# Windowed attention in the last two blocks: the softmax sums divided out of a tile's outputs instead of its weights

## The chip, the cores and the metric

The kernel runs on one core of one Trainium2 chip. The metric is the device time of one execution in microseconds (us); a time given for the kernel is a median over runs. The core has five engines that each work through a queue of their own strictly in program order and wait for one another on semaphores: TensorE (PE: matmuls, and transposes, which are matmuls against an identity matrix; its weight loads are shown apart as PEld), VectorE (DVE), ScalarE (ACT), GpSimd (POOL) and SyncE (SP, which only issues DMAs here). Matmuls write to PSUM, eight banks of 128 x 512 floats; DVE and ACT read it from there.

## What is computed

The reference is a decoder of six sublayers on `x` of 4 x 512 tokens and 256 channels (an RWKV-like mixer, a quantised fusion with a context, a mixture of experts, linear attention, cross-attention, and last a stack of two windowed-attention blocks), each followed by a residual sum and a layer norm. The change touches the attention in the two blocks of the last sublayer alone. There, for each block, in short:

```python
h = shift_token(x)                       # the upper half of the channels comes from the token before
q, k, v = split(h @ wqkv, 3)             # 8 heads of 64
q = l2norm(q) * qs;  k = l2norm(k) * ksc
q, k = rotary_xpos(q, k)
sim = einsum('bhwid,bhwjd->bhwij', 8.0 * bq, bk)   # windows of 128 tokens, own keys and those of the window before
sim = where((i < j) | (i > j + 128) | (j == -1), -max, sim)
out = einsum('bhwij,bhwjd->bhwid', softmax(sim), bv)
x = x + out @ wo
... # then a gated feed-forward network (the FFN), not touched
```

A softmax divides each row of exponentials by its sum. The division may be made on the weights (128 queries x 256 keys for each head) or, since the sum belongs to a query alone, on the outputs (128 queries x 64 channels for each head).

## The kernel before

`windowed` runs the two blocks (layers) one after the other; in each, `windowed_attention` comes first and `gated_ffn` after it. The 2048 tokens are 16 tiles of 128, which is also the window; a tile is named by a unit `u` (0 to 7) and `w` (0 or 1), and `n = 2u + w` counts tiles. Tiles 0, 4, 8 and 12 begin a sequence and have no window before them: they are called alone, and their scores, exponentials, flips and combines are half as long.

The order is one list, `windowed_plan`, which all engines walk, each doing its own share of every step. `mingle(main, side)` spreads the `side` steps evenly over the `main` steps, by their counts alone. For a unit the main steps are, tile by tile, `score`, the `flip` of the tile before, `softmax`, the `combine` of the tile before, and the `output` of the tile before that; the side steps are the rotations of the next unit (`rotate`, `scale`, `turn` for q and k of both tiles) and the projections of the unit after (`project` for q, k and v of both tiles, `split`, `invert`). The steps:

- `project` (L3333 on PE, six matmuls into a bank): ACT copies the bank out (L3543). For the k part (`which == 1`) ACT also squares q and k (L3549), and DVE then sums the squares (L3441, called the reduce below).
- `invert`: ACT takes the root (L3553), for which it loads a function table and then loads that of Exp again; DVE takes the reciprocal (L3445, L3447). `rotate` is DVE's L3458 and L3461 (with POOL's share L3619, L3620), `scale` is DVE's L3469, `turn` is four transposes on PE (L3342), which ACT copies out (L3563 for k, L3568 for q). `split` is a shift on DVE (L3432) and two casts on ACT.
- `score`: PE puts the mask into banks 0 to 3 (L3354) and adds q times k (L3361). There is one set of these banks: the scores of a tile wait until ACT has read those of the tile before.
- `softmax`: DVE takes the maxima (L3480, L3482), two groups of four heads one after the other; ACT takes eight exponentials and their sums (L3580); DVE then takes the reciprocals of the sums (L3488) and scales the weights (L3491), again in two groups.
- `flip`: PE transposes the weights, sixteen blocks into four banks (L3373), and ACT and DVE copy two banks each (L3516). `combine`: PE multiplies by v, 64 channels of a head against 128 queries (L3388), and ACT copies the result into `oc` (L3594). `output`: PE multiplies `oc` by wo (L3398), and DVE adds to `x_tok` (L3502).

Banks 4 to 7 go round in the order of the plan among `project`, `turn`, `flip`, `combine` and `output` (and, near the end of a layer, the first steps of the FFN): each use waits until the use four places back has been copied out. A copy that comes late on ACT or DVE therefore holds up PE at a step that has nothing else to do with it.

Of the kernel before, what the change touches and what calls it, by code (L numbers as in the profile page):

```python
# [9 lines left out]
ALU = mybir.AluOpType  # L10
# [3 lines left out]
P = 128  # L14
# [14 lines left out]
HL, NL = 8, 64  # L29
# [3129 lines left out]
WU, UNITS_W = 2, TILES // 2  # L3159
# [5 lines left out]
def windowed_plan():  # L3165
# [20 lines left out]
    for u in range(UNITS_W):  # L3186
        main = []
        for w in range(WU):
            n, before, after = WU * u + w, [], []
            if n == LAST_W - 2:  # L3190
                before, after = GATED_FIRST[0:1], GATED_FIRST[1:2]
            elif n == LAST_W:
                before = GATED_FIRST[2:3]
            main += [("score", u, w)] + tail[0:1] + before + [("softmax", u, w)] + after + tail[1:2] + last
            last, tail = tail[2:], [("flip", u, w), ("combine", u, w), ("output", u, w)]
        rotations = rotate(u + 1) if u + 1 < UNITS_W else []
        projections = project(u + 2) if u + 2 < UNITS_W else []
        plan += mingle(main, mingle(rotations, projections))
# [53 lines left out]
def windowed_attention(m, layer, f, fs, f_use, outer):  # L3252
    nc = m.nc
    with ExitStack() as ctx:
# [15 lines left out]
        for p in plan:  # L3270
            if p[0] in ("project", "turn", "combine", "output"):
                steps.append(p)
            elif p in GATED_FIRST:
                steps += ffn_uses([p])
            elif p[0] == "flip":
                steps += [p + (g,) for g in range(len(flips(*p[1:])))]
            elif p[0] == "score":
                for x in range(2):
                    use[p + (x,)] = Use(m, 2 * x)
# [34 lines left out]
def attention_pe(m, s, t, use, plan, layer, outer, fs, f):  # L3314
    pe = m.nc.tensor
    for step in plan:
# [48 lines left out]
        elif kind == "flip":  # L3365
            w, = step[2:]
            n = WU * u + w
            for g, blocks in enumerate(flips(u, w)):
                b = use[step + (g,)]
                pe.wait_ge(*s.weighed(2 * n + blocks[0][0] // 4 + 1))  # L3370
                pe.wait_ge(*b.empty)
                for i, (x, kk) in enumerate(blocks):
                    ins = pe.transpose(b.ap[:, i * P:(i + 1) * P], t["p"][n % 2][:, x, kk * P:(kk + 1) * P], m.const("ident"))  # L3373
                ins.then_inc(*b.fill)
        elif kind == "combine":
            w, = step[2:]
# [41 lines left out]
def attention_dve(m, s, t, use, plan, layer, outer, fs, f):  # L3418
# [3 lines left out]
    for step in plan:  # L3422
# [47 lines left out]
        elif kind == "softmax":  # L3470
            w, = step[2:]
            n, lo = WU * u + w, alone(u, w) * P
            peak, total, p = t["peak"][n % 2], t["total"][n % 2], t["p"][n % 2]
            scores = m.psum[:, 0:4, :].rearrange("p b (x j) -> p (b x) j", x=2)[:, :, lo:2 * P]
# [8 lines left out]
            if n >= LAST_W - 2:  # L3483
                ffn_dve(m, fs, f, use, GATED_FIRST[n - LAST_W + 2:n - LAST_W + 3], layer)
            for x in range(2):
                h = slice(4 * x, 4 * x + 4)
                v.wait_ge(*use["score", u, w, x].done)
                v.reciprocal(total[:, h], total[:, h]).then_inc(*s.v_step.up())  # L3488
                v.wait_ge(*s.v_step.now())
                for i in range(4 * x, 4 * x + 4):  # L3490
                    ins = v.tensor_scalar(p[:, i, lo:2 * P], p[:, i, lo:2 * P], total[:, i:i + 1], None, ALU.mult)  # L3491
                ins.then_inc(*s.weighed.up())
        elif kind == "flip":
# [25 lines left out]
def attention_act(m, s, t, use, plan, layer, outer, fs, f):  # L3519
    act = m.nc.scalar  # L3520
    for step in plan:
# [47 lines left out]
        elif kind == "softmax":  # L3569
# [3 lines left out]
            if n > 1:  # L3573
                before = (n - 2) // WU, (n - 2) % WU
                act.wait_ge(*s.weighed(2 * (n - 1)))
                act.wait_ge(*use[("flip",) + before + (len(flips(*before)) - 1,)].full)
# [8 lines left out]
        elif kind == "flip":  # L3585
            w, = step[2:]
            flip_out(m, t, use, u, w, 0)
        elif kind == "combine":
            w, = step[2:]
# [365 lines left out]
```

## Time and profile before

| what | us |
|---|---|
| time, median of 3 runs | 2553.82 |
| lowest and highest of them | 2547.07, 2555.61 |
| the profiled execution, its time | 2555.11 |
| the profiled execution, its span (first to last instruction) | 2553.8 |
| of the span: attention of layer 0, first scores to last output | 258 |
| of the span: attention of layer 1, the same | 262 |

The span is cut into stages that follow one another; the two attention stages together are about a fifth of it. The FFN of a layer begins when its attention has ended, but for three small steps. A row of the timeline gives the start, the busy time, the engine, the line of the code, what is written and read, how many instructions are merged into the row, and in brackets how long the engine sat idle before it and what ended that. A start-to-start distance between rows of an engine that is not waiting is what a step costs; matmuls are pipelined, so the busy times of neighbouring PE rows overlap a little.

### The profile page before, as it was taken

What the parts mean: (1) busy time and instruction counts of PE and PEld (TensorE: products, weight loads), DVE (VectorE), ACT (ScalarE), POOL (GpSimd) and SP (SyncE); (2) the same over time, 40 slices, a digit from 0 to 9 for tenths busy, and PEclk for the clock granted to TensorE, in tenths of its full rate; (3) what the DMA queues carried; (4) which work ended last, traced back from release to release, by engine and by line L of the source; (5) the groups of instructions that cost most, each with busy time, mean ns of one, the idle gap of its engine ahead of it and who ended that gap; (6) DMA issues with size and microseconds to landing.
All of it is one profiled execution on the core that took longest, in us unless ns stands there. A gap on an engine that the chain in (4) does not pass through costs nothing. (4 is left out here: it accounts for less than half of the span.)

```text
span 2553.8 us, 45980 instructions
## 1 busy us (share of the span) xinstructions
PE 2060.4 (81%) x17234; PEld 1349.0 (53%) x17337; DVE 1710.5 (67%) x3403; ACT 1198.9 (47%) x2235; POOL 857.0 (34%) x673
## 2 busy tenths in 40 slices
PE   5886579986589994777798989877887887787877
PEld 3555157873479983443244444444555544555544
DVE  5875977768956665666677777737777435777553
ACT  2232866646333332322255555546665434666442
POOL 1110034331056661012276768553221223221141
PEclk8986789999689997888899999988999998998999
DMA  4211034451351113332322322011000001000000
GB/s 147 56 48 44 1 92 131 141 167 50 132 219 51 49 46 113 89 84 84 85 76 73 90 77 69 24 51 61 1 1 1 25 1 52 1 1 1 34 9 25
DMA packets 107467, 159.65 MB, mean 63 GB/s; under 512 B 26064, under 2 KB 85236, under 8 KB 104180
## 3 DMA queue, kind: packets, MB, share of 16 engines
q1 hardware_dynamic: 102836, 144.64, 18.5%
q0 software_dynamic: 4416, 12.06, 1.6%
q8 instruction: 144, 2.36, 0.4%
q14 instruction: 71, 0.58, 0.1%
HBM read 109.42 MB, written 47.19 MB: 61 GB/s over the span
## 5 line engine op out<-in xcount | busy, mean ns | idle before, releaser
L3016 DVE TENSOR_REDUCE xa_max<-psum 128x1 f32<-128x1024 f32 (+1 forms) x256 | 246.3, 987 | 94.0 <-PE psum L2927 89.3
L3099 ACT ACTIVATE xa_work<-psum 128x1024 f32<-128x1024 f32 (+1 forms) x208 | 212.9, 1025 | 185.8 <-PE psum L2950 174.4
L3156 POOL TENSOR_TENSOR xa_ctx_f<-xa_ctx_f,xa_work 128x1024 f32<-128x1024 f32 x96 | 226.9, 2364 | 44.2 <-ACT xa_work L3099 36.8
L3333 PE MATMUL psum<-xa_c_parts,x_hl_f 128*128 128x512 bf16 x536 | 138.7, 403 | 62.0 <-ACT qk_raw_l L3543 20.6
L2927 PE MATMUL psum<-xa_key_rows,xa_query_rows 96*128 96x512 bf16 (+1 forms) x512 | 131.9, 350 | 29.1 <-DVE xa_max L3016 15.4
L2967 PE MATMUL psum<-xa_work,xa_values 128*32 128x128 f32 (+1 forms) x3328 | 141.1, 287 | 0.0
L1087 POOL TENSOR_TENSOR text_q<-text_q 128x512 bf16<-128x512 f32 x64 | 81.1, 1270 | 177.0 <-ACT text_q L1505 176.6
L2950 PE MATMUL psum<-xa_query_rows,xa_key_rows 98*128 98x512 bf16 (+1 forms) x416 | 130.4, 396 | 11.2 <-DVE xa_max L3016 11.2
L3580 ACT ACTIVATE w_p_l<-psum,w_max_l 128x256 f32<-128x256 f32 (+1 forms) x256 | 110.6, 459 | 56.4 <-DVE w_max_l L3482 56.4
L1837 PE MATMUL psum<-moe_rows,moe_w 128*128 128x256 bf16 x1104 | 130.3, 276 | 4.9 <-issue 4.9
L2096 ACT CAST x_ch<-moe_raw 128x512 bf16<-128x512 f32 x92 | 56.9, 618 | 158.9 <-DVE moe_raw L2011 149.7
L1850 PE MATMUL psum<-moe_w,x_ch 128*128 x1104 | 124.1, 273 | 0.0
L3333 PEld LDWEIGHTS psum<-xa_c_parts,x_hl_f 128*128 128x128 bf16 x576 | 55.4, 102 | 127.2 <-issue 26.0
L2967 PEld LDWEIGHTS psum<-xa_work,xa_values 128*32 128x32 f32 (+1 forms) x3328 | 83.0, 112 | 74.5 <-issue 72.6
L1837 PEld LDWEIGHTS psum<-moe_rows,moe_w 128*128 x1104 | 109.1, 99 | 18.8 <-issue 5.5
L1850 PEld LDWEIGHTS psum<-moe_w,x_ch 128*128 128x128 bf16 x1104 | 108.0, 98 | 12.5
L1353 PE MATMUL psum<-ctx_f,probs_t 128*128 128x128 f32 (+1 forms) x832 | 105.2, 286 | 9.9 <-issue 5.1
L1353 PEld LDWEIGHTS psum<-ctx_f,probs_t 128*128 128x128 f32 (+1 forms) x832 | 100.8, 200 | 12.1 <-issue 5.6
L3850 POOL TENSOR_TENSOR hidden_f<-h_act_f,hidden_f 128x512 bf16<-128x512 f32 (+1 forms) x48 | 55.4, 1155 | 147.7 <-ACT hidden_f L3823 147.7
L2011 DVE TENSOR_SCALAR moe_raw<-psum,cols 128x256 f32<-128x256 f32 x184 | 80.0, 477 | 23.2 <-PE psum L1837 17.8
L2927 PEld LDWEIGHTS psum<-xa_key_rows,xa_query_rows 96*128 96x128 bf16 x512 | 43.0, 101 | 98.5 <-DVE xa_max L3016 26.2
L3398 PE MATMUL psum<-wo_l,w_oc_l 128*128 128x256 f32 x256 | 75.4, 446 | 20.8 <-ACT w_q_l L3568 11.7
(484 smaller groups left out, 5015.4 us busy)
## 6 DMA issues: line engine op xcount, KB each, us to landing
text_q<-in_moe_w SPq DMA_DIRECT2D x64, 256.0 KB, 3.5
experts<-text_q SPq DMA_DIRECT2D x64, 256.0 KB, 2.8
moe_w<-experts SPq DMA_DIRECT2D x16, 1024.0 KB, 8.9
xa_key_rows<-cross_keys SPq DMA_DIRECT2D x48, 200.1 KB, 3.4
ctx_chunk<-in_ctxT SPq DMA_DIRECT2D x24, 300.0 KB, 3.0
cross_keys<-xa_k_hl SPq DMA_DIRECT2D x6, 800.5 KB, 3.7
moe_w<-pairs_out SPq DMA_DIRECT2D x8, 512.0 KB, 7.5
xa_ctx_f<-in_ctxT SPq DMA_DIRECT2D x4, 800.5 KB, 5.1
```

What stands on the lines that cost most here:

```text
L1087: g.tensor_tensor(parts[:, 1, :], t["expert_raw"][i % 2], parts[:, 0, :], ALU.subtract).then_inc(*s.e_low.up())
L1353: ins = pe.matmul(u.ap[:, 0:P], t["turned"][i % 2][0:rows, kt, :], t["values"][0:rows, n // TPB, kt, :], start=(kt == 0), stop=(kt == KT - 1))
L1837: ins = pe.matmul(u.ap[:, a * SLOT:(a + 1) * SLOT], w1[:, w, h, cf], t["x"][j % 2][:, x, h, :], start=(h, k) == (0, 0), stop=(h, k) == (1, 2))
L1850: ins = pe.matmul(u.ap[:, a * D:(a + 1) * D], t["hidden"][j % 2][:, x, f, q], w2[:, w, f, :], start=(f, k) == (0, 0), stop=(f, k) == (7, 2))
L2927: ins = pe.matmul(u.wide[:, x - c0:y - c0], t["q_rows"][n % 3][0:SPLIT, a, qt * P:(qt + 1) * P], t["k_rows"][n % 3][0:SPLIT, a, x:y], star ...
L2950: ins = pe.matmul(u.wide[0:rows, a * T:(a + 1) * T], t["k_rows"][n % 3][:, a, kt * P:kt * P + rows], t["q_rows"][n % 3][:, a, :], start=Tr ...
L2967: ins = pe.matmul(total.ap[lane:lane + NX, c:c + PIECE], t["v"][b][0:rows, kt, first + a, :], exps[0:rows, a, q:q + PIECE], start=(kt == 0 ...
L3016: v.tensor_reduce(t["maxes"][n % 2][:, qt * HU + a, part:part + 1], u.wide[:, 0:c1 - c0], AX.X, ALU.max).then_inc(*u.free)
L3099: act.activation(t["exps"][k % EXPS][0:rows], u.wide[0:rows].rearrange("p (m q) -> p m q", q=T), ACT.Exp, scale=1.0 / float(np.sqrt(np.flo ...
L3156: g.tensor_tensor(total, other, exps, ALU.add).then_inc(*s.added.up())
L3333: ins = pe.matmul(b.ap, x[:, i, h, w * P:(w + 1) * P], t["wqkv"][:, j, h, cols], start=(h, n) == (0, 0), stop=(h, n) == (1, 2))
L3580: ins = act.activation(t["p"][n % 2][:, i, lo:2 * P], scores[:, i, :], ACT.Exp, bias=t["peak"][n % 2][:, i:i + 1], scale=8.0, accum_out=t[ ...
```

## The change

The scaling of the weights (L3491) goes. Instead there is a new step, `norms`, after the `flip` of a tile and ahead of the next tile's `softmax`: DVE takes the reciprocals of the eight sums in one instruction, PE spreads them with eight matmuls (a column of reciprocals, repeated 64 times, against the identity) over 64 channels x 128 queries for each head, and ACT copies that bank into `oc`. At `combine` DVE multiplies the bank of outputs by `oc`, in place; ACT no longer copies there. `flip` now waits for ACT's exponentials, not for DVE. The new step takes a bank of the four that go round, and the main list of a unit has twelve steps in place of ten, so `mingle` lays the side steps between them differently.

```diff
-            main += [("score", u, w)] + tail[0:1] + before + [("softmax", u, w)] + after + tail[1:2] + last
-            last, tail = tail[2:], [("flip", u, w), ("combine", u, w), ("output", u, w)]
+            main += [("score", u, w)] + tail[0:2] + before + [("softmax", u, w)] + after + tail[2:3] + last
+            last, tail = tail[3:], [("flip", u, w), ("norms", u, w), ("combine", u, w), ("output", u, w)]
...
-            if p[0] in ("project", "turn", "combine", "output"):
+            if p[0] in ("project", "turn", "norms", "combine", "output"):
                 steps.append(p)
...
                 b = use[step + (g,)]
-                pe.wait_ge(*s.weighed(2 * n + blocks[0][0] // 4 + 1))
+                pe.wait_ge(*use["score", u, w, blocks[0][0] // 4].done)
                 pe.wait_ge(*b.empty)
...
+        elif kind == "norms":
+            w, = step[2:]
+            n, b = WU * u + w, use[step]
+            pe.wait_ge(*s.weighed(n + 1))
+            pe.wait_ge(*b.empty)
+            for p in range(4):
+                for x in range(2):
+                    share = t["total"][n % 2][:, 4 * x + p:4 * x + p + 1].to_broadcast([P, NL])
+                    ins = pe.matmul(b.ap[NL * x:NL * (x + 1), p * P:(p + 1) * P], share, m.const("ident"), start=True, stop=True)
+            ins.then_inc(*b.fill)
...
+        elif kind == "norms":
+            w, = step[2:]
+            total = t["total"][(WU * u + w) % 2]
             for x in range(2):
-                h = slice(4 * x, 4 * x + 4)
                 v.wait_ge(*use["score", u, w, x].done)
-                v.reciprocal(total[:, h], total[:, h]).then_inc(*s.v_step.up())
-                v.wait_ge(*s.v_step.now())
-                for i in range(4 * x, 4 * x + 4):
-                    ins = v.tensor_scalar(p[:, i, lo:2 * P], p[:, i, lo:2 * P], total[:, i:i + 1], None, ALU.mult)
-                ins.then_inc(*s.weighed.up())
+            v.reciprocal(total[:], total[:]).then_inc(*s.weighed.up())
+        elif kind == "combine":
+            w, = step[2:]
+            n, b = WU * u + w, use[step]
+            oc = t["oc"][n % 2][:].rearrange("p c t -> p (c t)")
+            v.wait_ge(*use["norms", u, w].done)
+            v.wait_ge(*b.full)
+            v.tensor_tensor(oc, b.ap, oc, ALU.mult).then_inc(*b.free)
...
-                act.wait_ge(*s.weighed(2 * (n - 1)))
+                act.wait_ge(*use[("norms",) + before].full)
...
-        elif kind == "combine":
+        elif kind == "norms":
             w, = step[2:]
             n, b = WU * u + w, use[step]
             if n > 1:
```

How the queues move is shown at one place, the second half of unit 3 of layer 0 (the time of tile 7, in which tile 6 is flipped and combined). In the names a digit is the buffer and `_l0` the layer; lines after L3190 are higher by up to 15 in the changed kernel.

DVE, from the copies of tile 6's flips to behind the maxima of tile 7 (`w_pt` flipped weights, `w_max` maxima, `w_sum` sums, `qk_norm` the reduce), before:

```order
L3516 COPY w_pt0_l0<-psum 128x512 x2
L3431 MEMSET x_shifted_l0 128x1
L3432 COPY x_shifted_l0<-x_ch 128x255
L3480 TENSOR_REDUCE w_max1_l0<-psum 128x4
L3482 TENSOR_SCALAR w_max1_l0<-w_max1_l0 128x4
L3480 TENSOR_REDUCE w_max1_l0<-psum 128x4
L3482 TENSOR_SCALAR w_max1_l0<-w_max1_l0 128x4
L3488 RECIPROCAL w_sum1_l0<-w_sum1_l0 128x4
L3491 TENSOR_SCALAR w_p1_l0<-w_p1_l0,w_sum1_l0 128x256 x4
L3488 RECIPROCAL w_sum1_l0<-w_sum1_l0 128x4
L3491 TENSOR_SCALAR w_p1_l0<-w_p1_l0,w_sum1_l0 128x256 x4
L3441 TENSOR_REDUCE qk_norm2_l0<-qk_sq_f0 128x16
```

and now:

```order
L3531 COPY w_pt0_l0<-psum 128x512 x2
L3479 TENSOR_TENSOR qk_rot4_l0<-qk_rot4_l0,qk_norm1_l0 128x512
L3441 MEMSET x_shifted_l0 128x1
L3442 COPY x_shifted_l0<-x_ch 128x255
L3500 RECIPROCAL w_sum0_l0<-w_sum0_l0 128x8
L3451 TENSOR_REDUCE qk_norm2_l0<-qk_sq_f0 128x16
L3490 TENSOR_REDUCE w_max1_l0<-psum 128x4
L3492 TENSOR_SCALAR w_max1_l0<-w_max1_l0 128x4
L3490 TENSOR_REDUCE w_max1_l0<-psum 128x4
L3492 TENSOR_SCALAR w_max1_l0<-w_max1_l0 128x4
L3507 TENSOR_TENSOR w_oc0_l0<-psum,w_oc0_l0 128x512
```

The eight scalings and their two reciprocals are gone from behind the maxima; one reciprocal stands ahead of them, and so does the reduce, which stood behind them; the multiplication into `w_oc` is new. The `scale` of the rotation (L3479) now stands behind the copies.

ACT, from the cast of the shifted half to the copy of a turned q (`qk_raw` the projected q or k, `qk_sq` their squares, `w_p` the exponentials, `w_k` and `w_q` the turned k and q), before:

```order
L3533 CAST x_hl_f0<-x_shifted_l0 128x256
L3568 COPY w_q0_l0<-psum 128x4x128
L3580 ACTIVATE w_p1_l0,w_sum1_l0<-psum,w_max1_l0 128x256 x8
L3543 COPY qk_raw1_l0<-psum 128x512
L3549 ACTIVATE qk_sq_f0<-qk_raw1_l0 128x1024
L3563 COPY w_k1_l0<-psum 128x4x128
L3594 COPY w_oc0_l0<-psum 128x512
L3568 COPY w_q0_l0<-psum 128x4x128
```

and now:

```order
L3548 CAST x_hl_f0<-x_shifted_l0 128x256
L3609 COPY w_oc0_l0<-psum 128x512
L3583 COPY w_q0_l0<-psum 128x4x128
L3558 COPY qk_raw1_l0<-psum 128x512
L3564 ACTIVATE qk_sq_f0<-qk_raw1_l0 128x1024
L3595 ACTIVATE w_p1_l0,w_sum1_l0<-psum,w_max1_l0 128x256 x8
L3578 COPY w_k1_l0<-psum 128x4x128
L3583 COPY w_q0_l0<-psum 128x4x128
```

The copy of the projected k and the squares moved from behind the exponentials to ahead of them, and the copy into `w_oc` too; the copy of the turned k (`w_k`) is now the first thing behind the exponentials.

PE, from the scores of tile 7 to the first matmuls of tile 6's combine (`xa_c_parts` the weights of the projections), before:

```order
L3361 MATMUL psum<-w_k0_l0,w_q1_l0 128x256 x8
L3373 MATMUL psum<-const,w_p0_l0 128x128 x16
L3342 MATMUL psum<-const,qk_rot1_l0 128x128 x4
L3333 MATMUL psum<-xa_c_parts,x_hl_f0 128x512 x6
L3342 MATMUL psum<-const,qk_rot2_l0 128x128 x4
L3388 MATMUL psum<-w_pt0_l0,w_v2_l0 64x128 x2
```

and now:

```order
L3361 MATMUL psum<-w_k0_l0,w_q1_l0 128x256 x8
L3373 MATMUL psum<-const,w_p0_l0 128x128 x16
L3383 MATMUL psum<-const,w_sum0_l0 64x128 x8
L3342 MATMUL psum<-const,qk_rot1_l0 128x128 x4
L3333 MATMUL psum<-xa_c_parts,x_hl_f0 128x512 x6
L3342 MATMUL psum<-const,qk_rot2_l0 128x128 x4
L3398 MATMUL psum<-w_pt0_l0,w_v2_l0 64x128 x2
```

The spreading matmuls (L3383) stand between the flips and the next turn and projection.

## Rows read from the trace of the kernel before

**Rows 1.** Windows: layer 0's attention, and four us of it; PEclk is the granted clock.

```profile
core 0: us, PE busy (x) PEld busy (x) DVE busy (x) ACT busy (x) POOL busy (x), PEclk, DMA share, GB/s
1742.00:2000.00 258.00, 199.52 (x1505) 141.41 (x1523) 187.03 (x402) 158.94 (x428) 51.31 (x66) 0.93 0.00 1
...
1898.00:1902.00 4.00, 3.11 (x8) 1.87 (x10) 2.53 (x6) 3.53 (x6) 0.00 (x0) 0.50 0.00 0
```

**Rows 2.** Timeline of PE, unit 3 of layer 0.

```profile
1839.49 1.03 PE L3354 MATMUL psum<-mask_b_l,ident_b_l 128*128 128x512 bf16 x4
1842.43 1.97 PE L3373 MATMUL psum<-const,w_p_l 128*128 128x128 f32 x16
1844.45 2.54 PE L3333 MATMUL psum<-xa_c_parts,x_hl_f 128*128 128x512 bf16 x11
1846.91 1.97 PE L3388 MATMUL psum<-w_pt_l,w_v_l 128*64 128x128 f32 x32
...
1854.19 1.03 PE L3354 MATMUL psum<-mask_b_l,ident_b_l 128*128 128x512 bf16 x4
...
1857.07 1.97 PE L3373 MATMUL psum<-const,w_p_l 128*128 128x128 f32 x16
...
1867.92 1.47 PE L3333 MATMUL psum<-xa_c_parts,x_hl_f 128*128 128x512 bf16 x6 [2.67 <-ACT qk_raw_l L3543]
1869.62 1.97 PE L3398 MATMUL psum<-wo_l,w_oc_l 128*128 128x256 f32 x8 [0.23 <-ACT w_k_l L3563]
...
1871.86 0.60 PE L3354 MATMUL psum<-mask_b_l,ident_b_l 128*128 128x256 bf16 x4
```

**Rows 3.** Timeline of all engines, the same unit: DVE and ACT around tile 6.

```profile
1845.78 0.59 ACT L3543 COPY qk_raw_l<-psum 128x512 f32<-128x512 f32 x1 [1.20 <-PE psum L3333]
...
1848.59 0.47 ACT L3580 ACTIVATE w_p_l<-psum,w_max_l 128x256 f32<-128x256 f32 x1 [2.22 <-DVE w_max_l L3482]
...
1850.56 0.18 DVE L3488 RECIPROCAL w_sum_l<-w_sum_l 128x4 f32<-128x4 f32 x1 [0.76 <-ACT w_p_l L3580]
...
1850.77 1.14 DVE L3491 TENSOR_SCALAR w_p_l<-w_p_l,w_sum_l 128x256 f32<-128x256 f32 x4
...
1852.20 0.62 ACT L3543 COPY qk_raw_l<-psum 128x512 f32<-128x512 f32 x1
...
1852.91 1.06 ACT L3549 ACTIVATE qk_sq_f<-qk_raw_l 128x1024 f32<-128x1024 f32 x1
...
1854.06 1.22 DVE L3441 TENSOR_REDUCE qk_norm_l<-qk_sq_f 128x16 f32<-128x1024 f32 x1 [0.33 <-ACT qk_sq_f L3549]
...
1861.32 0.29 DVE L3432 COPY x_shifted_l<-x_ch 128x255 f32<-128x255 f32 x1
```

**Rows 4.** Timeline of DVE and of ACT, unit 5: copies, scale, maxima, first exponential.

```profile
1908.63 1.50 DVE L3516 COPY w_pt_l<-psum 128x512 f32<-128x512 f32 x2
1910.04 0.69 DVE L3469 TENSOR_TENSOR qk_rot_l<-qk_rot_l,qk_norm_l 128x512 f32<-128x512 f32 x1
1910.65 1.21 DVE L3480 TENSOR_REDUCE w_max_l<-psum 128x4 f32<-128x1024 f32 x1
...
1912.18 0.47 ACT L3580 ACTIVATE w_p_l<-psum,w_max_l 128x256 f32<-128x256 f32 x1 [0.81 <-DVE w_max_l L3482]
```

**Rows 5.** Timeline of PE: after long waits, and where units 5 and 6 begin.

```profile
1898.89 2.34 PE L3333 MATMUL psum<-xa_c_parts,x_hl_f 128*128 128x512 bf16 x5 [5.01 <-ACT qk_raw_f L3543]
1901.03 3.19 PE L3398 MATMUL psum<-wo_l,w_oc_l 128*128 128x256 f32 x8
...
1904.48 1.03 PE L3354 MATMUL psum<-mask_b_l,ident_b_l 128*128 128x512 bf16 x4
...
1936.85 0.60 PE L3354 MATMUL psum<-mask_b_l,ident_b_l 128*128 128x256 bf16 x4
...
1988.94 3.68 PE L3398 MATMUL psum<-wo_l,w_oc_l 128*128 128x256 f32 x8 [3.00 <-ACT w_oc_l L3594]
```

**Rows 6.** Timeline of weight loads around a combine in unit 3.

```profile
1846.91 1.73 PEld L3388 LDWEIGHTS psum<-w_pt_l,w_v_l 128*64 128x64 f32 x32 [0.42 <-issue]
```

More of the change, by code:

```diff
@@ L3472, in attention_dve @@
             n, lo = WU * u + w, alone(u, w) * P
-            peak, total, p = t["peak"][n % 2], t["total"][n % 2], t["p"][n % 2]
+            peak = t["peak"][n % 2]
             scores = m.psum[:, 0:4, :].rearrange("p b (x j) -> p (b x) j", x=2)[:, :, lo:2 * P]
```

## The prediction, made blind

> **What bounds the kernel now.** The change lies in the two attention stages, so I read those first, as windows, and then one unit of them as a timeline, engine by engine. In layer 0's stage no engine is full: of 258 us PE is busy for 199.5, DVE for 187.0, ACT for 158.9 [rows 1]; layer 1 runs the same code again. A stage in which no engine is full is set by the waits between them, so what counts is the length of one turn round the loop and not a sum of busy times. A turn is a unit of two tiles. Unit 3 goes from the scores of tile 6 to those of tile 8, 1839.49 to 1871.86: 32.37 us, and its two halves are 17.58 (to the flips at 1857.07, behind the scores of tile 7) and 14.79 [rows 2]. Units 5 and 4 are 32.37 and 32.62 [rows 2, 5].
>
> The reader is to see three things in that unit. The scores of tile 7 (1854.19) come only behind ACT's last exponential of tile 6 (over at 1852.20, where the copy behind it starts), since they need the banks that the exponentials empty [rows 2, 3]. A single reduce (L3441) waits for ACT's squares, 1852.91 to 1854.06 [rows 3]. And the flips do not wait for DVE's scaling: at 1857.07 they follow the scores without an idle bracket, some 3.4 us after DVE has ended its second group (a reciprocal and 1.14 of scaling behind that last exponential) [rows 2, 3]. So the wait that the change takes from `flip` is worth nothing directly; its worth is the time that DVE wins.
>
> **What the change removes.** On DVE, for each tile, two reciprocals (0.21 from start to start) and two groups of four scalings (1.14): 2.70 us busy, and the waits for ACT between them, 0.76 ahead of the first [rows 3]: some 3.9 us in which DVE could not go on. It adds one reciprocal (0.21) and one multiplication of 512 columns out of PSUM: the nearest rows are the flips' copies out of PSUM (1.50 for two) and a product of the same size in SBUF (0.69) [rows 4], so 0.7. DVE wins about 3 us a tile. For ACT nothing is added: one copy of 512 columns has another bank as its source.
>
> **What it adds on PE.** Eight f32 matmuls with 64 output channels and 128 columns. No such row exists; the nearest are the combine's sixteen of that very shape, 1.97 us [rows 2], so 0.98 a tile. Not below: the columns are the same; above by what the change of shape costs. Around a combine the weight loads show a bracket of 0.42 and PE itself shows none [rows 2, 6]; so each tile may lose up to 0.84 more, at the entry and at the exit.
> The Trainium skill, TensorEngine Tiling (Array Packing), Key Properties, says that a switch of the tiling mode, and not merely of the tile, drains TensorE; the new matmuls are two more such switches a tile. The trace agrees as far as the 0.42 goes, and shows no wait of PE for it.
>
> **What it moves, and what decides.** The twelve main steps shift the side steps between them. In units 1 to 4, in both halves, the k projection with its squares and reduce now stands ahead of `softmax` on every engine, where it stood behind. And PE reaches this projection only behind the new matmuls, which wait for DVE's reciprocal, which stands behind DVE's share of the flips and a `scale`. So a chain that was loose becomes one string, and I lay it out from rows of unit 3 and 5.
>
> First half, from the start of the scores of tile 6: flips begin 2.94 later [rows 2]. From there DVE copies two banks and scales, until it is free 3.22 later (1907.43, which is 2.95 behind 1904.48, to 1910.65, in unit 5, where that order stands already) [rows 4, 5]; in the kernel before the maxima begin here, at 6.16. Now: reciprocal 0.21, a semaphore 0.1 (an estimate), spreading 0.98, projection until ACT can copy 1.33 (1844.45 to 1845.78), copy 0.71, squares 1.15, reduce 1.22 [rows 2, 3]: the maxima begin at 11.86. Then 1.53 to the first exponential [rows 4], 3.61 for eight of them (1848.59 to 1852.20) [rows 3], and 2.4 for half of the masks and the scores (of 2.88 from 1854.19 to 1857.07) [rows 2]: 19.40 against 17.58, **1.8 us worse**.
>
> Second half, from the flips of tile 6: 3.22, shift 0.29, reciprocal 0.21, 0.1, spreading 0.98, a turn 0.49 (a quarter of the flips' 1.97), then 1.33, 0.71, 1.15, 1.22, 1.53 and 3.61 as above: the exponentials end at 14.84 [rows 2 to 4]. Ahead of the next scores PE still has `output` and one turn. The bank for `output` is that of a turned k, whose copy now stands behind the exponentials on ACT: 0.62. Then 2.24 (1869.62 to 1871.86) [rows 2]: 17.70 against 14.79, **2.9 worse**. What DVE wins does not help: it would sit idle for the squares some 4.7 us in this half.
>
> PE's own work in that half (turn, projection, turn, combine, turn, projection) is over near 10.8, so it waits 4.6 us before `output`. Rows: behind a wait of 5.01 the granted clock was 0.50 in the four us from 1898, which is 1.2 GHz and not 2.4 [rows 1, 5]; `output` took 3.19 there and 3.68 behind a wait of 3.00, but 1.97 soon after one of 2.67 [rows 2, 5]. So 1.2 to 1.7 more; I take 1.4. Unit 3 becomes 38.5, 6.1 worse.
>
> **The sum.** Units 1 and 3: 6.1 each. Units 2 and 4 begin with an alone tile, whose exponentials and flips are shorter; with two thirds of 5.14 for maxima to last exponential and one copy in place of two I estimate 17.9 and 16.8, so 34.7 against 32.62, and 1.4 for the clock: 3.5 each. Unit 5 keeps its first reduce behind the maxima: there PE's new 0.98 and 0.3 of waiting count, 1.3; its second half is that of unit 3, 2.9, and 1.4: 5.6. Units 0, 6 and 7 have no such string in both halves, and DVE's 3 us a tile tell: I estimate gains of 2, 1 and 0. A layer: 12.2 + 7.0 + 5.6 - 3 = 21.8 us; two layers 43.6. On the span of 2553.8 this gives 2597.4. The profiled execution's own time is 1.3 above its span, and the median of the runs shown, 2553.82, is that span almost exactly; so the forecast for the median is **2597 us**, slower by 1.7%. Ends: without the clock's 1.4 (five units, two layers, 14 us) 2583; with 0.84 a tile for the switches on ten tiles a layer, 17 us more, 2614.
>
> **The rivals.** *DVE's relief decides (faster).* If the maxima could begin where DVE comes free, as now 6.2 to 6.4 us behind the scores, and not behind the squares, units 1 to 5 would be bound by PE. PE's work in a stage is 199.5, and 15.7 come (16 tiles by 0.98); if some 25 us of waits stay in units 0, 6 and 7, a stage takes 240 and not 258: 36 us for both, 2518. For it: DVE is the fuller of the two engines that empty banks. Against it: the order, in which the reduce stands ahead of the maxima. It decides if the squares of a half are ready less than about 1 us after DVE's reciprocal, where I reckon 4.3 (0.1, 0.98, 1.33, 0.71 and 1.15, added).
> *It evens out (same).* First halves lose 1.8, but the second ones win as much, since DVE arrives early with its rotations, and units 0, 6 and 7 pay for the new matmuls: 2554, give or take 8. Against it: in the second half DVE's rotations are not in the string at all.
> *The clock holds (slower, less).* PE's waits of 4.6 us don't lower it: 2583.
> *The new matmuls cost double (slower, more).* They are 0.98 by shape; at twice that, or with the drains above, 2614. The string passes through them once a half.
> *The change does not do what it says.* It does remove the scalings; there is no second path by which they come back.
>
> **How the numbers follow.** The forecast, 0.50; the clock holds, 0.20; costlier matmuls or drains, 0.10; together 0.80 for slower by over 0.3%, which is about what a measurement of this kernel can tell from no change. Even, 0.08. Faster, 0.12. The range reaches from a forecast without clock and with half of unit 5's and the alone units' loss struck out, 2566, to 2618, just above the costly case; what is left out are the two cases that are not slower.
>
> **What would show it.** In the trace of the changed kernel: in units 1 to 4 the reduce (L3451) idle before it for ACT's squares, by 2 to 3 us in first halves and 4 to 5 in second ones, directly ahead of the maxima (L3490), which begin near 11.9 us behind the scores; PE waiting for DVE's reciprocal ahead of L3383, 0.3 us in first halves and about 2 in second ones; PE waiting some 4.6 us ahead of `output` for a `w_k` copy, and that `output` near 3.2 or more; units of 37 to 39 us, and of 35 to 37 where they begin alone. L3383 should take about 1 us for eight. The forecast is wrong if units 1 to 5 come out at 32 us or less; the step that then failed is the string through the spreading matmuls, unless these matmuls themselves take a time far from 0.98.

## The result, and the profile after

The changed kernel takes 2617.03 us (median of four runs, 2610.98 to 2618.96). Its ratio to the kernel before, run beside it, is 1.0255, 95% interval [1.0236, 1.0274]: slower by 65 us. On the 2553.82 of the kernel before that is 2618.9, just above the upper end of the forecast's range, 2618; the four runs' own median lies just below it. Direction and mechanism were right, the size (43.6) was a third too small.

The profiled execution took 2618.22, with a span of 2616.9, 63.1 above that of before. From the first masks of layer 0's attention to those of layer 1's it grew by 33.6, from there to the end by 27.6; 1.9 lie ahead of both. Units 1 to 5 alone grew by 37.4 in layer 0 and by 33.2 in layer 1, so the loss is in the two attention stages.

Windows of the kernel before, units 1 to 5 of layer 0, from the masks of one unit to those of the next; the columns are length, then busy time of each engine, then the granted clock (PEclk):

```profile
1774.32:1806.73 32.41, 26.88 (x220) 18.96 (x221) 25.05 (x52) 21.81 (x57) 7.80 (x10) 1.00 0.01 2
1806.73:1839.49 32.76, 25.83 (x180) 17.94 (x181) 23.28 (x51) 20.13 (x55) 7.68 (x10) 0.90 0.00 1
1839.49:1871.86 32.37, 26.88 (x220) 18.95 (x221) 25.31 (x53) 21.57 (x56) 7.80 (x10) 1.00 0.00 1
1871.86:1904.48 32.62, 25.68 (x179) 17.81 (x180) 23.28 (x51) 20.13 (x55) 7.68 (x10) 0.90 0.00 1
1904.48:1936.85 32.37, 26.80 (x218) 19.03 (x220) 25.54 (x51) 20.97 (x54) 6.60 (x8) 1.00 0.00 1
```

The same of the changed kernel, and behind the dots the two halves of its unit 3, parted where the flips of tile 6 begin:

```profile
1773.54:1816.15 42.61, 33.69 (x249) 23.03 (x252) 21.62 (x37) 22.21 (x56) 7.46 (x10) 0.86 0.01 1
1816.15:1854.03 37.88, 28.16 (x211) 19.57 (x213) 19.62 (x34) 20.55 (x55) 6.89 (x10) 0.91 0.00 1
1854.03:1895.19 41.16, 32.24 (x251) 22.89 (x252) 21.05 (x36) 22.10 (x56) 7.43 (x10) 0.92 0.00 1
1895.19:1932.78 37.59, 27.81 (x212) 19.26 (x213) 19.59 (x35) 20.55 (x55) 6.90 (x10) 0.91 0.00 1
1932.78:1973.44 40.66, 32.10 (x251) 23.01 (x252) 21.93 (x35) 21.28 (x54) 6.09 (x8) 0.92 0.00 1
...
1854.03:1873.74 19.71, 17.86 (x152) 11.85 (x151) 13.61 (x23) 12.19 (x29) 2.80 (x4) 1.00 0.00 1
1873.74:1895.19 21.45, 14.38 (x101) 11.04 (x101) 7.45 (x13) 9.91 (x27) 4.62 (x6) 0.84 0.00 2
```

DVE (third of the busy times) lost 3 to 4 us a unit, as it should, and every unit got 5 to 10 us longer. In units 1, 3 and 5 the clock, full before, fell to 0.86 to 0.92; in units 2 and 4 it was at 0.90 already.

TensorE's timeline in unit 3, to be laid beside [rows 2]; a row gives start, busy time, line, and in brackets the idle time ahead of it with what ended it:

```profile
1860.43 1.09 PE L3383 MATMUL psum<-const,w_sum_l 128*64 128x128 f32 x16 [0.20 <-DVE w_sum_l L3500]
...
1873.74 1.97 PE L3373 MATMUL psum<-const,w_p_l 128*128 128x128 f32 x16
1877.88 1.98 PE L3383 MATMUL psum<-const,w_sum_l 128*64 128x128 f32 x16 [2.17 <-DVE w_sum_l L3500]
1879.78 1.12 PE L3342 MATMUL psum<-const,qk_rot_l 128*128 128x128 f32 x4
1881.12 1.30 PE L3333 MATMUL psum<-xa_c_parts,x_hl_f 128*128 128x512 bf16 x5 [0.22 <-issue]
...
1891.26 3.56 PE L3408 MATMUL psum<-wo_l,w_oc_l 128*128 128x256 f32 x8 [4.63 <-ACT w_k_l L3578]
1895.19 0.60 PE L3354 MATMUL psum<-mask_b_l,ident_b_l 128*128 128x256 bf16 x4
```

All waits that were foretold are there: 0.20 and 2.17 us for the reciprocal, 4.63 ahead of `output` for the bank of the turned k. What was not foretold: behind the first long wait the eight spreading matmuls take 1.98 and not 1.09, and the turn 1.12 and not 0.6. Behind the second, `output` takes 3.56 and not the 1.97 of [rows 2]; that was foretold (3.2 or more).

VectorE in the same unit, with the reduce and the first maximum of the first half, and of the second:

```profile
1864.79 1.22 DVE L3451 TENSOR_REDUCE qk_norm_l<-qk_sq_f 128x16 f32<-128x1024 f32 x1 [3.13 <-ACT qk_sq_f L3564]
1865.93 1.22 DVE L3490 TENSOR_REDUCE w_max_l<-psum 128x4 f32<-128x1024 f32 x1
...
1884.21 1.22 DVE L3451 TENSOR_REDUCE qk_norm_l<-qk_sq_f 128x16 f32<-128x1024 f32 x1 [6.39 <-ACT qk_sq_f L3564]
1885.35 1.21 DVE L3490 TENSOR_REDUCE w_max_l<-psum 128x4 f32<-128x1024 f32 x1
```

The maxima of the first half begin 11.90 us behind its masks (11.86 forecast; 6.16 before), after VectorE sat idle 3.13 us for the squares. In the second half it sat idle 6.39, where 4 to 5 had been foretold.

### The profile page after: what moved, and what is told of

Read it like the earlier page. It is cut to its first block and busy times, and to the rows that moved or that the text cites. A ratio compares the mean times of both kernels' runs of the same rounds, so it can differ in the third digit from the quotient of the medians.

```text
span 2616.9 us, 46838 instructions
## 1 busy us (share of the span) xinstructions
PE 2102.3 (80%) x17740; PEld 1379.4 (53%) x17849; DVE 1652.3 (63%) x3147; ACT 1202.8 (46%) x2235; POOL 849.8 (32%) x673
## 3 DMA queue, kind: packets, MB, share of 16 engines
q1 hardware_dynamic: 102836, 144.64, 18.1%
## 5 line engine op out<-in xcount | busy, mean ns | idle before, releaser
L3333 PE MATMUL psum<-xa_c_parts,x_hl_f 128*128 128x512 bf16 x530 | 134.1, 391 | 19.5 <-POOL x_hl_f L3623 6.5
L3451 DVE TENSOR_REDUCE qk_norm_l<-qk_sq_f 128x16 f32<-128x1024 f32 x32 | 39.0, 1219 | 115.0 <-ACT qk_sq_f L3564 115.0
```

What stands on the lines that cost most here:

```text
L3333: ins = pe.matmul(b.ap, x[:, i, h, w * P:(w + 1) * P], t["wqkv"][:, j, h, cols], start=(h, n) == (0, 0), stop=(h, n) == (1, 2))
```

## The experiments

Two theories stood against each other. A: the loss comes from where the steps now stand, a string through reciprocal, projection, squares, reduce, maxima and exponentials, with TensorE's clock falling in the waits. B: it is the price of the new matmuls and of their wait itself. The last column is the ratio less one, times 2553.82. Each diff shows the lines that matter; dots stand for the others.

| kernel | median us | ratio, 95% interval | us against before |
|---|---|---|---|
| changed | 2617.03 | 1.0255 [1.0236, 1.0274] | +65 |
| old order, new arithmetic | 2552.64 | 1.0016 [1.0006, 1.0025] | +4 |
| new order, old arithmetic | 2589.29 | 1.0152 [1.0135, 1.0169] | +39 |
| changed, early reciprocal | 2582.36 | 1.0127 [1.0110, 1.0144] | +32 |
| changed, wait filled | 2610.07 | 1.0244 [1.0223, 1.0264] | +62 |
| changed, both waits filled | 2615.04 | 1.0238 [1.0213, 1.0264] | +61 |
| changed, turned k copied first | 2577.09 | 1.0080 [1.0059, 1.0101] | +20 |
| changed, reduce behind maxima | 2569.56 | 1.0069 [1.0052, 1.0086] | +18 |
| changed, early reciprocal and k first | 2535.72 | 0.9920 [0.9901, 0.9939] | -20 |
| the same, reduce behind maxima too | 2531.29 | 0.9916 [0.9899, 0.9932] | -21 |
| old order, early reciprocal | 2536.57 | 0.9928 [0.9909, 0.9947] | -18 |
| the same, spreading matmuls twice | 2547.10 | 0.9964 [0.9947, 0.9980] | -9 |
| old order, early reciprocal, late reduce | 2523.21 | 0.9885 [0.9868, 0.9901] | -29 |

### Order and arithmetic apart

The old order under the new arithmetic; flips and norms count as one main step:

```diff
...
-            last, tail = tail[3:], [("flip", u, w), ("norms", u, w), ("combine", u, w), ("output", u, w)]
+            last, tail = tail[2:], [[("flip", u, w), ("norms", u, w)], [("combine", u, w)], [("output", u, w)]]
...
```

> The changed kernel with one thing undone: flips and norms count as one main step, so that ten and not twelve main steps of a unit are laid among the side steps, and the k projection of each half stands behind the maxima again, as before; the new arithmetic stays. Theory A (the loss comes from the order: projection, squares and reduce ahead of the maxima, and the clock that falls behind the waits this makes): units 1 and 3 of layer 0 take 31 to 34.5 us instead of 42.6 and 41.2, the maxima no longer wait for the squares, and the time is 2535 to 2575. Theory B (the loss is the new matmuls and the wait for the reciprocal themselves, 32 tiles by 1 to 2 us): the time stays at 2590 to 2620, with units 1 to 5 of 36 us and more.

Units 1 to 4 of layer 0 take 33.7 to 34.0 us, and 61 of the 65 us are gone: theory A. Yet the new arithmetic then only breaks even. TensorE waits for the reciprocal in both halves of unit 3, and over all 32 tiles its spreading matmuls wait 44.6 us and their weight loads, at the same time, 52.2:

```profile
1847.66 1.09 PE L3383 MATMUL psum<-const,w_sum_l 128*64 128x128 f32 x16 [1.38 <-DVE w_sum_l L3500]
...
1864.29 1.09 PE L3383 MATMUL psum<-const,w_sum_l 128*64 128x128 f32 x16 [1.83 <-DVE w_sum_l L3500]
```

The other way round, the new order under the old arithmetic:

```diff
...
-            last, tail = tail[2:], [("flip", u, w), ("combine", u, w), ("output", u, w)]
+            last, tail = tail[3:], [("flip", u, w), ("nothing", u, w), ("combine", u, w), ("output", u, w)]
...
-    return plan + last + tail
+    return [step for step in plan + last + tail if step[0] != "nothing"]
```

> The kernel before, with weights scaled as before and no new matmul, but an empty main step where norms would stand, so that twelve main steps are counted and the side steps stand where the change puts them. Theory A (order): the reduce of the squares stands ahead of the maxima, which begin some 9.3 us behind a first half's scores instead of 6.2; up to 3 us on each half of units 1 to 5: 2585 to 2620, most of the loss without the new work. Theory B (new work): 2546 to 2562, as before.

39 us more than before: an empty entry in a list, with no instruction behind it, costs 1.5%. VectorE in the first half of unit 3, whose masks begin at 1843.97:

```profile
1853.33 1.22 DVE L3441 TENSOR_REDUCE qk_norm_l<-qk_sq_f 128x16 f32<-128x1024 f32 x1 [1.80 <-ACT qk_sq_f L3549]
1854.46 1.21 DVE L3480 TENSOR_REDUCE w_max_l<-psum 128x4 f32<-128x1024 f32 x1
```

The maxima begin 10.5 us behind the masks, against 6.2 before (9.3 had been expected), and in the second half `output` waits 5.29 for the copy of the turned k. Theory B is out as the main cause. The 39 us and the 4 us of the kernel with the old order leave 22 of the 65: these come only when the new order and the new arithmetic meet.

### The three links of the string, one at a time

The reciprocal ahead of VectorE's copies of the flips:

```diff
...
         elif kind == "norms":
             w, = step[2:]
-            total = t["total"][(WU * u + w) % 2]
-            for x in range(2):
-                v.wait_ge(*use["score", u, w, x].done)
-            v.reciprocal(total[:], total[:]).then_inc(*s.weighed.up())
+            pass
...
         elif kind == "flip":
             w, = step[2:]
+            total = t["total"][(WU * u + w) % 2]
+            for x in range(2):
+                v.wait_ge(*use["score", u, w, x].done)
+            v.reciprocal(total[:], total[:]).then_inc(*s.weighed.up())
             flip_out(m, t, use, u, w, 1)
```

> The changed kernel with one step moved: DVE takes the reciprocal of the sums ahead of its copies of the flips, not behind them and the shift. If the half rate behind TensorE's wait for the reciprocal is the term that was sized too small: that wait (2.2 us in second halves) falls under 0.7, the eight spreading matmuls take 1.1 there and not 2.0, unit 3 gets 2 to 3 us shorter, and the time is 2590 to 2603. If the string to the maxima does not run through the reciprocal there: 2611 to 2619.

It gains 33 us on the changed kernel, nearly 8 us more than the expectation's best case. TensorE in unit 3's second half:

```profile
1863.84 1.97 PE L3373 MATMUL psum<-const,w_p_l 128*128 128x128 f32 x16
1865.74 1.09 PE L3383 MATMUL psum<-const,w_sum_l 128*64 128x128 f32 x16
1866.76 0.66 PE L3342 MATMUL psum<-const,qk_rot_l 128*128 128x128 f32 x4
...
1877.92 3.49 PE L3408 MATMUL psum<-wo_l,w_oc_l 128*128 128x256 f32 x8 [5.00 <-ACT w_k_l L3579]
```

No wait, no half rate at the spreading matmuls, and a unit of 37.45 instead of 41.16. The wait before `output` stays, and so does the half rate behind it.

That wait in turn: ScalarE's copy of the first turned k ahead of the exponentials.

```diff
...
+    for i in range(len(plan) - 1):
+        if plan[i][0] == "softmax" and plan[i][2] == 1 and plan[i + 1] == ("turn", plan[i][1] + 1, 0, 1):
+            plan[i], plan[i + 1] = plan[i + 1], plan[i]
```

> The changed kernel with one step moved in units 1 to 5: ScalarE's copy of the first turned k (the copy that gives back the bank that `output` takes) stands ahead of the second half's exponentials and not behind them. Theory (the forecast's step: `output` waits for that copy, and TensorE falls to half rate in the wait): in unit 3 `output` then waits for VectorE's product with the spread reciprocals, done 15.0 us behind the flips and not 17.1, the wait of 4.6 becomes 2 to 2.5, the next masks come 2.3 to 3.9 us earlier, and the time is 2575 to 2595. Rival (the bank is taken late anyway, and the string of squares, maxima and exponentials alone sets the length): 2608 to 2619.

It gains 45 us, near the best that the theory expects. `output` no longer waits at all, where the expectation still had 2 to 2.5 us, and runs at the full rate; the next masks wait 0.99 for the exponentials, which now end last:

```profile
1876.98 1.89 PE L3412 MATMUL psum<-wo_l,w_oc_l 128*128 128x256 f32 x8
...
1881.20 0.39 PE L3358 MATMUL psum<-mask_b_l,ident_b_l 128*128 128x256 bf16 x2 [0.99 <-ACT w_p_l L3599]
```

The reduce behind the maxima, on VectorE alone:

```diff
...
+    for i in range(len(plan) - 1):
+        if plan[i][0] == "project" and plan[i][3] == 1 and plan[i + 1][0] == "softmax":
+            plan[i], plan[i + 1] = plan[i + 1], plan[i]
```

> The changed kernel with one step moved on VectorE alone: the reduce of the squares stands behind the maxima, not ahead of them, in units 1 to 5; projection, copies and squares stay where the change put them on TensorE and ScalarE. Theory A (the forecast's string, squares, reduce, maxima, exponentials, sets each half): the maxima run while ScalarE squares, the exponentials follow the squares at once and start up to 2.6 us earlier (1.22 for the reduce, 1.5 from maxima to exponential), nine halves of a layer by up to 2.6: 2570 to 2590. Theory B (the bank of `output`, the wait for the reciprocal and the clock behind them set the length): 2600 to 2619.

It gains 47 us: theory A, at the best end of its range. In unit 3's second half the maxima now follow the reciprocal at once and the reduce waits by itself:

```profile
1861.92 1.17 DVE L3494 TENSOR_REDUCE w_max_l<-psum 128x4 f32<-128x1024 f32 x1
...
1868.47 1.22 DVE L3455 TENSOR_REDUCE qk_norm_l<-qk_sq_f 128x16 f32<-128x1024 f32 x1 [3.32 <-ACT qk_sq_f L3568]
```

So each of three single moves takes back half or more of the loss, and their sum, 125, is nearly twice it, so they are not three separate shares of it. That they are links of one string is argued from the rows: where one is cut, waits shrink on other engines too. Two of them together:

> The changed kernel with both single steps moved: the reciprocal ahead of VectorE's copies, and ScalarE's copy of the first turned k ahead of the exponentials. The side steps stay where the change put them. Theory A (the two losses are separate places in a unit, and add up): 34 us from the first and 20 to 35 from the second, so 2548 to 2565 against 2617. Theory B (one hides the other, as the clock gave back in one wait was lost in the next): 2575 to 2585, as with the early reciprocal alone.

They add up, and more (33 and 45, measured 85), to 20 us below the kernel before and below theory A's range, with the side steps where the change put them. These two lie at separate places of a unit. The third move on top:

> The changed kernel with three single moves and its side steps left in place: VectorE's reciprocal ahead of its copies, ScalarE's copy of the first turned k ahead of the exponentials, VectorE's reduce behind the maxima. With the first two alone it took 2536, with TensorE waiting 0.3 and 1.1 us for each half's exponentials. Theory A (the reduce is what still holds the maxima): TensorE bounds the halves at 15 to 16 us and not 16.3 to 16.9, 2500 to 2522. Theory B (ScalarE's projection copy and squares ahead of its exponentials hold them as long): 2528 to 2540.

Theory B held: the interval overlaps that without it. Once the first two were cut, the reduce was worth a few us at most.

### The clock

Transposes of no use fill the wait for the reciprocal in second halves:

```diff
...
+            if w == 0 and 1 <= u <= 5:
+                for i in range(16):
+                    pe.transpose(b.ap[:, (i % 4) * P:(i % 4 + 1) * P], m.const("ident"), m.const("ident"))
             pe.wait_ge(*s.weighed(n + 1))
```

> The changed kernel, with 16 transposes of the identity (16 of this shape take 1.97 us at the full rate) put into the bank of the spreading matmuls ahead of the wait for the reciprocal, in the second halves of units 1 to 5; they change no result. If the clock is what makes the spreading matmuls and the turn behind that wait long: these take 1.1 and 0.5 us instead of 1.98 and 1.12, the projection starts some 1.4 us earlier, and the time falls by 10 to 20 us, to 2597 to 2607. If they are long for another reason (the shape of the matmul, the switch between them): 2615 to 2625, since the transposes fill a wait and no more.

Windows of the changed kernel, unit 3, behind its two long waits (granted clock third from the end):

```profile
1878.00:1880.00 2.00, 2.00 (x17) 1.67 (x18) 0.00 (x0) 0.20 (x2) 1.77 (x3) 0.50 0.00 0
...
1891.20:1893.20 2.00, 1.94 (x5) 1.59 (x6) 0.00 (x0) 0.89 (x2) 0.00 (x0) 0.57 0.00 0
1893.20:1895.20 2.00, 2.00 (x9) 1.50 (x9) 0.27 (x1) 0.00 (x0) 0.00 (x0) 0.58 0.00 0
```

and of the filled one, the same places:

```profile
1867.00:1869.00 2.00, 1.79 (x21) 1.53 (x23) 0.10 (x1) 1.06 (x3) 1.50 (x3) 1.00 0.00 0
...
1878.90:1880.90 2.00, 1.94 (x5) 1.61 (x6) 0.00 (x0) 0.89 (x2) 0.00 (x0) 0.50 0.04 8
1880.90:1882.90 2.00, 2.00 (x7) 1.54 (x6) 0.08 (x1) 0.00 (x0) 0.00 (x0) 0.50 0.00 0
1882.90:1884.90 2.00, 2.00 (x16) 1.41 (x16) 0.35 (x1) 1.28 (x2) 0.00 (x0) 0.63 0.00 0
```

The first spell at 1.2 GHz (0.50) is gone, but the second is longer and reaches into the next unit. TensorE in the same half:

```profile
1863.02 1.97 PE L3373 MATMUL psum<-const,w_p_l 128*128 128x128 f32 x16
...
1868.88 1.24 PE L3333 MATMUL psum<-xa_c_parts,x_hl_f 128*128 128x512 bf16 x5
...
1878.96 3.75 PE L3411 MATMUL psum<-wo_l,w_oc_l 128*128 128x256 f32 x8 [4.62 <-ACT w_k_l L3581]
```

The projection starts 5.86 behind the flips and not 7.38, 1.5 us earlier as foretold, and `output` at 15.94 and not 17.52. Part of that is lost again: from `output` to the next masks it takes 4.40 us and not 3.93, and the next masks and scores start slower. Unit 3 won 0.8 us, and the interval of the whole overlaps that of the changed kernel: in time, neither theory's range was met. A last run filled the end of the second wait too:

```diff
...
+            if w == 1 and u <= 4:
+                pe.wait_ge(*use["score", u + 1, 1, 0].done)
+                for i in range(10):
+                    pe.transpose(m.psum[:, 0, (i % 4) * P:(i % 4 + 1) * P], m.const("ident"), m.const("ident"))
```

> The changed kernel with the transposes ahead of the wait for the reciprocal as before, and ten more ahead of `output` in the second halves of units 1 to 5, into a bank of scores that the first four exponentials have read; they run in the last 2.5 us of the wait of 4.6 and change no result. With the first filled alone the half rate behind that wait went, and the one at `output` lasted longer. Theory A (the clock at the two places is what the forecast sized too small): `output` takes 2.0 to 2.9 us and not 3.56 to 3.75, the unit gains another 1 to 1.7 us, and the time is 2590 to 2604. Theory B (the half rate is only put off to whatever follows, or the transposes run at half rate and delay `output` as much as they help): 2605 to 2622.

Theory B of that expectation, and the two layers show both of its ways. The ten transposes and `output`, unit 3 of layer 0, then of layer 1:

```profile
1884.59 2.34 PE L3412 MATMUL psum<-const 128*128 128x128 f32 x10 [2.33 <-ACT w_p_l L3602]
1886.80 2.59 PE L3415 MATMUL psum<-wo_l,w_oc_l 128*128 128x256 f32 x8
...
2327.16 1.28 PE L3412 MATMUL psum<-const 128*128 128x128 f32 x10 [2.33 <-ACT w_p_l L3602]
2329.37 3.78 PE L3415 MATMUL psum<-wo_l,w_oc_l 128*128 128x256 f32 x8 [0.93 <-ACT w_k_l L3585]
```

Either the transposes run at half rate and `output` recovers some, or they run at the full rate and `output` has the half rate all the same. Filler bought nothing here that can be measured in the time of the kernel; taking the waits away bought 33 and 45 us.

### The new matmuls, and the best order

> The new arithmetic in the old order of side steps, and the reciprocal taken ahead of VectorE's copies. With the old order alone TensorE still waited 97 us in all for the reciprocal, 1.4 and 1.8 us in the two halves of unit 3, and its units took 33.9 us. Theory A (that wait is on the path, since a half of 16.2 us has TensorE at work all the rest of it): units of 30.5 to 32 us, 2505 to 2530, faster than before. Theory B (something else takes the wait's place): 2540 to 2556.

The 97 us of this expectation add the matmuls' waits and the weight loads', which pass together; it is 44.6 us of TensorE's time. The kernel comes out 18 us under the kernel before, between the two theories. TensorE's waits in the second half of unit 3 remained:

```profile
1858.36 1.09 PE L3383 MATMUL psum<-const,w_sum_l 128*64 128x128 f32 x16 [1.61 <-DVE w_sum_l L3510]
...
1865.79 1.47 PE L3333 MATMUL psum<-xa_c_parts,x_hl_f 128*128 128x512 bf16 x6 [1.54 <-ACT qk_raw_l L3559]
```

In that kernel the eight spreading matmuls were then issued twice (`for p in [0, 1, 2, 3] * 2`):

> The kernel with the old order and the early reciprocal, its eight spreading matmuls of a tile issued twice. It measures what they cost by themselves. If they lie on TensorE's path at the time of their rows, 0.98 a tile on 32 tiles: 25 to 38 us above the kernel with them once. If half of them lie in waits: 8 to 20. If a switch of shape costs beside them what no row shows: no more than with the first theory, since the switch comes once in either kernel.

The lines of costliest groups, once and twice (busy time, mean ns, idle time before):

```profile
L3383 PE MATMUL psum<-const,w_sum_l 128*64 128x128 f32 x512 | 35.0, 279 | 19.4 <-DVE w_sum_l L3510 19.4
```

```profile
L3383 PE MATMUL psum<-const,w_sum_l 128*64 128x128 f32 x1024 | 62.9, 276 | 14.2 <-DVE w_sum_l L3510 13.3 <-ACT w_pt_l L3532 0.9
```

28 us more of TensorE's time cost some 9 us, with intervals that just touch: the second case of the expectation, in which half of it or more falls into waits. Last, VectorE's late arrival: the reduce of the first half was moved behind that half's product, rotation and scale (on VectorE, in the kernel with the old order and the early reciprocal).

```diff
...
+    for u in range(2, UNITS_W):
+        step, after = ("project", u, 0, 1), ("scale", u - 1, 1, 0)
+        if plan.index(step) < plan.index(after):
+            plan.remove(step)
+            plan.insert(plan.index(after) + 1, step)
```

> The kernel with the old order and the early reciprocal (2537), with one step moved on VectorE: the first half's reduce stands behind the product, the rotation and the scale of the same half, so that VectorE does these in the 4.3 us in which it waited for the squares. Theory A (the second half, 17.9 us, is held by VectorE, which comes to its flip copies and maxima 2 us late): second halves of 15.5 to 16.5, 2508 to 2522. Theory B (TensorE's wait there is for ScalarE's copy of the projection, which stands behind the exponentials anyway): 2530 to 2540.

2523 us, 0.9885 [0.9868, 0.9901] of the kernel before, the fastest here and the other way round from the change: theory A, if a microsecond above its range. Halves of 15.0 and 15.8 us in unit 3; the wait for the reciprocal in the second half is gone, one of 1.17 for the projection's copy stays:

```profile
1836.31 1.03 PE L3354 MATMUL psum<-mask_b_l,ident_b_l 128*128 128x512 bf16 x4
...
1851.35 1.03 PE L3354 MATMUL psum<-mask_b_l,ident_b_l 128*128 128x512 bf16 x4
...
1854.24 1.97 PE L3373 MATMUL psum<-const,w_p_l 128*128 128x128 f32 x16
1856.13 1.09 PE L3383 MATMUL psum<-const,w_sum_l 128*64 128x128 f32 x16
...
1863.20 1.47 PE L3333 MATMUL psum<-xa_c_parts,x_hl_f 128*128 128x512 bf16 x6 [1.17 <-ACT qk_raw_l L3565]
...
1867.14 0.60 PE L3354 MATMUL psum<-mask_b_l,ident_b_l 128*128 128x256 bf16 x4
```

## Why the prediction was right, and where it was not

**The cause was right.** The twelve counts, more than the matmuls, make the loss: undoing them takes 61 of 65 us away, and doing them alone costs 39. The other 22 come when the string also runs through the reciprocal and the spreading matmuls. The string exists as laid out: cutting it at the reciprocal, at the reduce, or at the bank of `output` takes back 33, 47 and 45.

**The first half of unit 3 was right**: 19.71 us against 19.40, its maxima at 11.90 against 11.86. No row stood behind the 0.1 for a semaphore; spreading starts 0.05 us behind the end of the reciprocal.

**The second half of unit 3 was forecast 2.35 us too short** (17.70 and 1.4 for the clock, 21.45 measured). The spreading matmuls begin 4.14 behind the flips (3.82 forecast; the shift took 0.75 and not the 0.29 of [rows 3]). From there to the projection it takes 3.24 (1877.88 to 1881.12), not the 1.47 of spreading and turn at the full rate. With the filler, at the full rate, it takes 1.73, so 1.5 us of it is half rate, in the middle of the string. The exponentials end at 16.75, not 14.84, and `output` begins at 17.52, not 15.46. From there to the next masks it is 3.93, against 3.64 with the forecast's 1.4.

So the step that failed is "I take 1.4", the clock's term: one spell of half rate a unit, put behind the wait of 4.6 alone, when the forecast itself had a wait of about 2 us for the reciprocal in the same half. The runs show 1.7 to 2.2 us behind the wait before `output` (3.92 to 4.40 to the next masks, where it is 2.24 at the full rate), and in five of the ten second halves a spell behind the wait for the reciprocal as well, which puts `output` 1.5 to 1.7 us later than in the filled kernel. That a wait shorter than 4.6 could matter was to be seen in [rows 5], where one of 3.00 was followed by an `output` of 3.68; the one of 2.67 in [rows 2] was not.

**The other units** by halves, parted at the flips behind the second tile's scores, layer 0; the forecast's second halves have the 1.4 in them:

| unit | forecast: first, second half | measured |
|---|---|---|
| 1 | 19.4, 19.1 | 20.6, 22.0 |
| 2 | 17.9, 18.2 | 18.4, 19.5 |
| 3 | 19.4, 19.1 | 19.7, 21.5 |
| 4 | 17.9, 18.2 | 18.3, 19.3 |
| 5 | 17.9, 20.1 | 18.1, 22.6 |

The five units are 12.7 us longer than forecast, 10 of that in the second halves. Some 8 are the clock by the spells above (an estimate from the rows), with 0.9 in unit 1's first half, whose masks take 1.91 and not 1.03, soon after a wait of 2.37. The rest are waits sized too small: in unit 5 the spreading matmuls begin 5.25 behind the flips, and in the alone units, estimated roughly, `output` begins 0.6 later than the forecast's 14.6. Units 0 and 6 came out at -2.6 and +0.7, where -2 and -1 had been put down. The lower end of the range, 2566, strikes out all of unit 5's loss without the clock; half of it, as the text says, gives 2570.

**Of the 33 us of the early reciprocal** the rows show most. In the filled kernel, with the wait but at the full rate, `output` begins 1.7 to 1.9 us later behind the flips than with the early reciprocal (15.94 against 14.08 in unit 3); the forecast's string gives 1.85. In ten second halves that is some 19 us. The half rate in five of them, 1.5 to 1.7 each, is another 8. Where the other 6 come from is open. And taking the half rate alone away is not worth these 8: the filler did that, and gained some 3 us that can't be told from none, since the next spell grew.

**The rivals.** *DVE's relief decides* was priced at 2518 on the condition that the maxima need not wait for the squares. In this kernel they do. In the old order with the early reciprocal they don't, and the time is 2537; with the late reduce as well it is 2523. The rival's sum came near in the end, but its condition was false here. *It evens out* gives the time of the new arithmetic in the old order (+4), not its mechanism: there the first half of unit 3 lost 1.5 (19.12 us) and the second won nothing (14.80). *The clock holds* is out: in the rows read, no `output` directly behind a wait of over 4 us ran at its full rate. *Matmuls that cost double* is out: at the full rate the eight take 1.03 from start to start, against 0.98, and doubled in fact, in the old order, they cost 9 us. On the switch of the array's shape no wait shows here: in the last kernel above the spreading matmuls start 1.89 us behind the start of the sixteen flips, and a turn of the flips' own shape started 1.80 behind it in the kernel before (1857.07 to 1858.87). So it is 0.1 a switch at most, not 0.42. The Trainium skill, TensorEngine Tiling (Array Packing), Key Properties, says that a switch of the tiling mode drains TensorE. *The change does not do what it says* is out by VectorE's busy time.

## What to carry to other kernels

Where a plan spreads side work by counting steps, a new step moves every step behind it: read the new order for what now stands ahead of the operation that all wait for, and price that before the arithmetic. A step put on an idle engine costs what its input waits for, so ask first where the producer of that input stands in its own queue; here the place of one 0.2 us reciprocal was worth 33 us. And a wait on TensorE should be priced with the slower matmuls that may follow it, each time it occurs, and not only behind the longest.

## What was not expected of the hardware

Waits of the same length were followed by different clocks: 2.17 us ahead of the spreading matmuls gave 1.98 us for them in unit 3 of layer 0, while in unit 1 of layer 1 they took 1.09 behind the same wait:

```profile
2243.63 1.09 PE L3383 MATMUL psum<-const,w_sum_l 128*64 128x128 f32 x16 [2.17 <-DVE w_sum_l L3500]
```

And 2 us of useless matmuls in such a wait took away the half rate behind it, but the spell behind the next wait grew from under 4 us to over 5.
